# The last feed-forward of a four-layer network as one stage, with its low-rank corrections as products of 32 rows

## The reference

```
even = lt[:, ::2, :]; odd = lt[:, 1::2, :]              # lt: tokens 1 to 16 of each batch
m1 = (even[:, :4, :, None] * odd[:, :4, None, :]).reshape(Bx, Hx, Dx)   # Hx = 1024, Dx = 256
m2 = (even[:, 4:, :, None] * odd[:, 4:, None, :]).reshape(Bx, Dx, Hx)
h = x @ W1.T + scale * einsum('bsd,bhd->bsh', x, m1) + b1
h = gelu(h, approximate=False)
out = h @ W2.T + scale * einsum('bsh,boh->bso', h, m2) + b2
```

## Time and profile before

| | us |
|---|---|
| median of 3 runs | 4879.96 (4879.55 to 4884.21) |
| profiled execution | 4880.05 |
| its span | 4878.3 |
| busy in the span: TensorE / VectorE / ScalarE / GpSimd | 4319.7 / 2473.7 / 1964.9 / 553.3 |

### The profile page before, as it was taken

How to read it: one execution, slowest core, us unless ns; L and a number is a source line. 1 busy time by engine, 2 the same in 40 slices (tenths; PEclk the granted TensorE clock), 3 DMA queues, 4 the chain that set the end, 5 groups by cost and what they waited for, 6 DMA issues and landing times. The chain is left out here.

```text
span 4878.3 us, 144357 instructions
## 1 busy us (share of the span) xinstructions
PE 4319.7 (89%) x65736; PEld 3428.9 (70%) x65736; DVE 2473.7 (51%) x4177; ACT 1964.9 (40%) x3848; POOL 553.3 (11%) x262
## 2 busy tenths in 40 slices
PE   7999996599999979999986789999962789999968
PEld 5877774488888858888853568777741668888844
DVE  4555553566666655545545445555525255555530
ACT  3554442233333334444432335455431244444421
POOL 1111111000000011111112011111102011111100
PEclk9999997599999989999988799999975899999989
DMA  2111100021111121111022011111012611111000
GB/s 69 43 36 43 36 23 16 24 77 49 49 49 49 39 63 37 37 44 37 31 54 53 19 52 43 36 43 36 30 25 84 224 57 38 41 40 38 24 20 19
DMA packets 89472, 223.14 MB, mean 46 GB/s; under 512 B 28736, under 2 KB 52307, under 8 KB 86147
## 3 DMA queue, kind: packets, MB, share of 16 engines
q1 hardware_dynamic: 85360, 209.06, 13.6%
q10 hardware_dynamic: 2736, 2.75, 0.2%
q0 software_dynamic: 768, 2.10, 0.1%
HBM read 196.16 MB, written 9.32 MB: 42 GB/s over the span
## 5 line engine op out<-in xcount | busy, mean ns | idle before, releaser
L690 DVE TENSOR_REDUCE x_pm<-banks 128x4 f32<-128x1536 f32 (+2 forms) x512 | 935.5, 1827 | 687.2 <-PE banks L591 687.2
L792 ACT ACTIVATE x_pl<-banks 128x384 f32<-128x384 f32 x1536 | 628.8, 498 | 710.1 <-PE banks L574 710.1
L516 POOL TENSOR_TENSOR x_cl<-xnT,x_ch 128x1601 fp32r<-128x1601 f32 x116 | 386.4, 3331 | 2171.9 <-ACT x_ch L807 2171.9
L797 ACT ACTIVATE x_kT<-banks,x_bk 128x384 f32<-128x384 f32 (+2 forms) x512 | 305.1, 596 | 530.9 <-PE banks L602 530.9
L614 PE MATMUL banks<-x_wh,x_ch 128*128 128x256 f32 (+1 forms) x1664 | 489.6, 294 | 0.0
L574 PE MATMUL banks<-x_q,x_kT 32*128 32x128 f32 x13312 | 481.8, 276 | 3.1 <-issue 3.0
L591 PE MATMUL banks<-x_kT,x_q 32*128 32x384 f32 (+2 forms) x4096 | 457.8, 512 | 14.0 <-DVE x_v L722 9.0
L614 PE MATMUL banks<-x_wh,x_cl 128*128 128x256 f32 (+1 forms) x1664 | 468.4, 281 | 0.0
L614 PE MATMUL banks<-x_wl,x_ch 128*128 128x256 f32 (+1 forms) x1664 | 467.0, 281 | 0.0
L602 PE MATMUL banks<-x_ch,x_wh 128*128 128x384 f32 (+2 forms) x1024 | 410.3, 401 | 43.7 <-DVE x_cl L773 43.1
L574 PEld LDWEIGHTS banks<-x_q,x_kT 32*128 32x128 f32 x13312 | 435.7, 184 | 6.9 <-issue 4.3
(11 more groups left out here) (339 smaller groups left out, 7010.5 us busy)
## 6 DMA issues: line engine op xcount, KB each, us to landing
xnT<-in_ctxT SPq DMA_DIRECT2D x120, 800.5 KB, 4.3
e_w<-in_L_pack SPq DMA_DIRECT2D x91, 384.0 KB, 3.1
e_w<-in_L_pack SPq DMA_DIRECT2D x21, 1154.0 KB, 7.8
a_swap<-a_raw SPq DMA_DIRECT2D x64, 128.0 KB, 2.3
actT<-in_ctxT SPq DMA_DIRECT2D x8, 800.5 KB, 4.9
e_rw<-routed_rows SPq DMA_DIRECT2D x64, 64.0 KB, 2.8
x_rows<-e_zero SPq DMA_DIRECT2D x1, 2688.0 KB, 9.6
e_xt<-x_rows ACTq DMA_DIRECT2D x3, 896.0 KB, 10.5
```

The lines of the kernel that those rows point to most:

```text
L516: nc.gpsimd.tensor_tensor(cl[:, u, k, 0:CTX], staged(b, k), ch[:, u, k, 0:CTX], ALU.subtract).then_inc(low_done, 1)
L690: nc.vector.tensor_reduce(pm[:, c, :, g], src[:, :, 0:hi - lo], AX.X, ALU.max).then_inc(max_done, 1)
L792: nc.scalar.activation(probabilities(c, j, lo, hi).rearrange("p t q -> p (t q)"), mine[j][:, 0:(hi - lo) * P], ACT.Exp).then_inc(exp_done, 1)
L797: nc.scalar.activation(kT[:, c, lo:hi], mine[1 if g == 0 and inside(b if c else b - 1) else 0][:, 0:hi - lo], ACT.Identity, bias=col[:, c: ...
```

## The change

The two stages and `project` are replaced by one, `lora_ffn`. Instead of 64 rows (all batches) per correction, the 8 batches of a half of the tokens take 32 rows, and four copies of these rows are held side by side in the 128 partitions, one for each of the four products that follow one another: four hidden chunks in the first correction, four token tiles in the second. Each copy meets another 32 rows of TensorE and another bank. The hidden tiles are done in four groups of four (half of the tokens, four chunks). The left side of the second correction is gathered tile by tile, in products that write 32 partitions each; its right side, e2, is made by products with columns of the identity instead of a strided copy. All transfers are issued at the start of the stage, and TensorE waits for the first weights alone before its first plain products. POOL clears two tiles of picks first, since VectorE fills only parts of them.

Left out below: VectorE makes four more picks for c1 after those for e1, and c1 itself as before (128 rows x 512 for each half, after e1); it then fills `pick_e2` and `pick_g` with 16 copies of 32 columns each, the second set behind the e2 drains; for each half it makes `gm` (128x128) and adds the finished tiles. TensorE waits for `g_taken` before the outputs of a half, and issues 4 transposes and 4 products of 512 columns at the start. The stores are as before.

```diff
-def project(net, tag, w, bias, chunks, extra, out):
-def lora_hidden(net, tag, gm, e2):
+def lora_ffn(net, tag, out):
...
+        pick_e1 = net.sb(tag + "_pe1", [P, 2, KC, P], ctx=mem)
+        pick_c = net.sb(tag + "_pc", [P, 2, KC, P], ctx=mem)
+        pick_e2 = net.sb(tag + "_pe2", [P, 2, 4, KC, P], ctx=mem)
+        pick_g = net.sb(tag + "_pg", [P, 2, 4, KC, P], ctx=mem)
...
+        def hidden_bank(h, g, x):
+            return net.bank(4 * (1 - g) + x)
+        def out_bank(t):
+            return net.bank(4 + t if t < 4 else (1, 2, 3, 4)[t - 4])[:, 0:D]
...
+        def _(sp):
+            sp.dma_start(w1[:], d["L3_ffn_W1T"].rearrange("(c p) n -> p c n", p=P)).then_inc(w1_in, 16)
+            sp.dma_start(b1[:], d["L3_ffn_b1"]).then_inc(table_in, 16)
+            sp.dma_start(scale[:], spread(d["L3_ffn_scale"], (P, 1))).then_inc(table_in, 16)
+            sp.dma_start(own[:], d["own_rows"]).then_inc(table_in, 16)
+            sp.dma_start(own8[:], d["own_tile"]).then_inc(table_in, 16)
+            sp.dma_start(m4[:], d["m4"]).then_inc(table_in, 16)
+            sp.dma_start(b2[:], spread(d["L3_ffn_b2"], (P, D))).then_inc(bias_in, 16)
+            sp.dma_start(w2[:], d["L3_ffn_W2T"].rearrange("(c p) n -> p c n", p=P)).then_inc(w2_in, 16)
...
+        def _(pool):
+            nc.gpsimd.memset(pick_e2[:], 0.0).then_inc(cleared, 1)
+            nc.gpsimd.memset(pick_g[:], 0.0).then_inc(cleared, 1)
+            pool.wait_ge(bias_in, 16)
+            for t in range(TILES):
+                nc.gpsimd.tensor_tensor(net.x[:, t, :], net.x[:, t, :], b2[:], ALU.add).then_inc(biased, 1)
...
+        def _(dve):
+            for h in range(2):
+                for c in range(KC):
+                    src = token_rows(c, 1, h).unsqueeze(1)
+                    nc.vector.tensor_copy(pick_e1[:, h, c].rearrange("p (x b i) -> p x b i", x=4, i=4),
+                                          spread(src, (P, 4, 8, 4))).then_inc(ev_picked, 1)
...
+            dve.wait_ge(table_in, 80)
+            dve.wait_ge(ev_made, 1)
+            for h in range(2):
+                for i in range(4):
+                    nc.vector.tensor_scalar(e1[:, h, i], net.bank(0)[:, h * D:(h + 1) * D], m4[:, i:i + 1], None,
+                                            ALU.mult).then_inc(e1_ready, 1)
...
+            for n, (pick, first, picked) in enumerate(((pick_e2, 9, e2_picked), (pick_g, 10, g_picked))):
+                dve.wait_ge(cleared, n + 1)
...
+                if n == 0:
+                    dve.wait_ge(e2_made, 1)
+                    for i in range(4):
+                        nc.vector.tensor_scalar(e2[:, :, i], net.bank(3)[:, 0:2 * S].rearrange("p (h j) -> p h j", h=2),
+                                                m4[:, i:i + 1], None, ALU.mult).then_inc(e2_ready, 1)
...
+        def _(pe):
+            def hidden(h, g):
+                for x in range(4):
...
+                    for k in range(KC):
+                        nc.tensor.matmul(hidden_bank(h, g, x), w1[:, k, c * P:(c + 1) * P],
+                                         net.xnT[:, k, h * HALF:(h + 1) * HALF], start=(k == 0), stop=False)
+                if h == g == 0:
+                    pe.wait_ge(e1_ready, 8)
+                    pe.wait_ge(c_taken, 2)
+                for x in range(4):
+                    c = 4 * g + x
+                    rows = slice(32 * x, 32 * x + 32)
+                    nc.tensor.matmul(hidden_bank(h, g, x), e1[rows, h].rearrange("p i d -> p (i d)")[:, c * P:(c + 1) * P],
+                                     c1[rows, h], start=False, stop=True).then_inc(made, 1)
+            def gates(h):
+                pe.wait_ge(taken, 8 * h + 8)
+                for r in range(4):
+                    for c in range(KC):
+                        for q in range(4):
...
+                            last = nc.tensor.matmul(net.bank(0)[rows, 0:P], pick_g[:, h, r, c, rows],
+                                                    net.actT[:, 2 * r + c, t * P:(t + 1) * P], start=(r == c == 0),
+                                                    stop=(r == 3 and c == KC - 1))
+                last.then_inc(g_made, 1)
+            def outputs(h):
...
+                    nc.tensor.matmul(out_bank(t), gm[rows, h], e2[rows, h].rearrange("p i j -> p (i j)"), start=True, stop=False)
+                for t in range(4 * h, 4 * h + 4):
+                    for c in range(8):
+                        last = nc.tensor.matmul(out_bank(t), net.actT[:, c, t * P:(t + 1) * P], w2[:, c], start=False, stop=(c == 7))
+                    last.then_inc(p_made, 1)
...
+            pe.wait_ge(ev_picked, 4)
...
+            pe.wait_ge(w1_in, 16)
+            hidden(0, 0)
+            pe.wait_ge(e2_picked, 16)
...
+                        last = nc.tensor.matmul(net.bank(3)[:, at:at + 32], pick_e2[:, h, r, c], net.ident[:, r:P:4],
+                                                start=(r == 0), stop=(r == 3))
+            last.then_inc(e2_made, 1)
+            pe.wait_ge(e2_ready, 4)
+            hidden(0, 1)
+            hidden(1, 0)
+            pe.wait_ge(g_picked, 16)
+            gates(0)
+            pe.wait_ge(g_taken, 1)
+            hidden(1, 1)
+            pe.wait_ge(w2_in, 16)
+            outputs(0)
+            gates(1)
+            outputs(1)
```

More of the change, by code:

```diff
@@ L2110, in lora_hidden @@
         b1 = net.sb(tag + "_b1", [P, 8], ctx=mem)
[L2111 to L2118, removed]
+        b2 = net.sb(tag + "_b2", [P, D], ctx=mem)
@@ new lines, in _ @@
+            for t in range(TILES):
+                sp.wait_ge(added, t + 1)
+                sp.dma_start(out[t * P:(t + 1) * P, :], net.x[:, t, :]).then_inc(stored, 16)
+            sp.wait_ge(stored, 16 * TILES)
+        @block.gpsimd
+        def _(pool):
+            nc.gpsimd.memset(pick_e2[:], 0.0).then_inc(cleared, 1)
+            nc.gpsimd.memset(pick_g[:], 0.0).then_inc(cleared, 1)
+            pool.wait_ge(bias_in, 16)
+            for t in range(TILES):
+                nc.gpsimd.tensor_tensor(net.x[:, t, :], net.x[:, t, :], b2[:], ALU.add).then_inc(biased, 1)
@@ new lines, in _ @@
+        @block.vector
+        def _(dve):
[6 more added lines that the diff above has]
+                for c in range(KC):
+                    src = token_rows(c, 2, h).unsqueeze(1)
+                    nc.vector.tensor_copy(pick_c[:, h, c].rearrange("p (x b i) -> p x b i", x=4, i=4),
+                                          spread(src, (P, 4, 8, 4))).then_inc(c_picked, 1)
+            dve.wait_ge(table_in, 80)
+            dve.wait_ge(ev_made, 1)
+            for h in range(2):
+                for i in range(4):
+                    nc.vector.tensor_scalar(e1[:, h, i], net.bank(0)[:, h * D:(h + 1) * D], m4[:, i:i + 1], None,
+                                            ALU.mult).then_inc(e1_ready, 1)
+            for h in range(2):
+                dve.wait_ge(c_made, h + 1)
+                nc.vector.scalar_tensor_tensor(c1[:, h], net.bank(1 + h), scale[:, 0:1], own[:], ALU.mult,
+                                               ALU.mult).then_inc(c_taken, 1)
+            for n, (pick, first, picked) in enumerate(((pick_e2, 9, e2_picked), (pick_g, 10, g_picked))):
+                dve.wait_ge(cleared, n + 1)
+                for h in range(2):
+                    for c in range(KC):
+                        for r in range(4):
+                            dst = pick[:, h, r, c].rearrange("p (q x) -> p q x", x=32)[:, :, 8 * r:8 * r + 8]
+                            src = token_rows(c, first, h).rearrange("p (q b) i -> p q b i", b=2)
+                            nc.vector.tensor_copy(dst.rearrange("p q (b i) -> p q b i", i=4), src).then_inc(picked, 1)
+                if n == 0:
[3 more added lines that the diff above has]
+                                                m4[:, i:i + 1], None, ALU.mult).then_inc(e2_ready, 1)
+            for h in range(2):
+                dve.wait_ge(g_made, h + 1)
+                nc.vector.scalar_tensor_tensor(gm[:, h], net.bank(0)[:, 0:P], scale[:, 0:1], own8[:], ALU.mult,
+                                               ALU.mult).then_inc(g_taken, 1)
+                for t in range(4 * h, 4 * h + 4):
+                    dve.wait_ge(p_made, t + 1)
+                    dve.wait_ge(biased, t + 1)
+                    nc.vector.tensor_tensor(net.x[:, t, :], net.x[:, t, :], out_bank(t), ALU.add).then_inc(added, 1)
@@ new lines, in gates @@
+            def gates(h):
+                pe.wait_ge(taken, 8 * h + 8)
+                for r in range(4):
+                    for c in range(KC):
+                        for q in range(4):
+                            t = 4 * h + q
+                            rows = slice(32 * q, 32 * q + 32)
+                            last = nc.tensor.matmul(net.bank(0)[rows, 0:P], pick_g[:, h, r, c, rows],
+                                                    net.actT[:, 2 * r + c, t * P:(t + 1) * P], start=(r == c == 0),
```

(47 more changed lines are left out.)

39 lines of the change are left out of this document (26 added, 13 removed).

## The result

| | us |
|---|---|
| the changed kernel, median of 4 runs | 4834.35 (4826.34 to 4836.19) |
| the kernel before, 4 runs beside it | 4882.09 (4879.55 to 4889.40) |
| ratio | 0.9901 (95% interval 0.9889 to 0.9913) |
| profiled execution after | 4833.99, span 4832.2 |

A forecast was written before the change was run, and what follows sets the result against it. TensorE's own instructions and holes were taken to bound the stage; 2.9 + 32.1 + 4.7 + 5.1 + 28.8 + 1.7 = 75.3 us against 126.4, so 4880 - 51 = 4829 us, range 4822 to 4840 (own range 4825 to 4834).

The forecast's parts named there:

- Step 1: Start of the stage: POOL's clears hold up VectorE's picks, so TensorE starts 2.9 us later than before.
- Step 2: Ahead of the first layer: TensorE's hole of 4.08 us goes, with the slow first four records (3.51 for 1.71).
- Step 3: Hidden tiles with packed 32-row corrections: 8.03 us a group, 32.1 us for four, where the old took 49.3.
- Step 4: Making e2 by thin products: 3.5 us, then 1.2 us waiting for VectorE's drains, 4.7 us in all.
- Step 5: Gathering the second correction's left side: twice 2.55 us, 5.1 in all, against 13.95 plus a hole of 9.42.
- Step 6: Outputs, second layer with its corrections: 14.4 us for each half, 28.8 in all, against 49.0.
- Step 7: Behind e2's thin products and their hole: one spell at the half clock, +1.7 us, bounds 0 and +5.
- Rival B: Narrow products of corrections and gathering overlap badly: 4851 us with nothing overlapped, 4840 with half; chance 0.17.
- C: TensorE gets the half clock for most of the stage: 4894 us with all work doubled; chance 0.01.
- Rival A: No blocking of picks at the start and no lost clock: 4824 us; chance 0.2.

The follow-up runs named there:

- e1: The changed kernel with POOL's two clears held back until VectorE has made its first eight picks; 4828.20 us, 0.9895 of the kernel before.
- e3: The changed kernel with TensorE's wait for the four e2 drains moved behind the plain products of three hidden tiles; 4830.99 us, ratio 0.9893.
- e2: The changed kernel with the four corrections of a hidden group all read from partitions 0 to 31, one row group; 4845.50 us, ratio 0.9924.
- e5: The changed kernel with each gathering group ordered token tile by token tile instead of the four tiles in turn; 4834.57 us, one run.
- e8: The changed kernel with its bias and second weights asked for only when the last hidden group is made; 4838.19 us, one run.
- e4: The kernel before, with only the second weights and their bias loaded in the first of the two stages; 4872.15 us, ratio 0.9975.

## Why the prediction was right, step by step

- **Step 1, start.** Forecast 2.9 us later than before, by POOL's clears. Measured: TensorE starts 3.86 us after the first pick instead of 1.00, 2.86 later; e1 shows that this was the clears, not the copies. The transposes and small products themselves took 6.11 us instead of 5.74, as the clock rose later (the granted clock was 0.50 for the first 4.1 us of them, before the change for about 3.3): +0.4, not forecast; in e1 they took 5.75.
- **Step 2, first hole.** Gone: plain products follow the small ones without idle time, and the tables (VectorE began at 4752.00) and c1 (done at 4756.5) were there 4.9 us before TensorE asked at 4761.4.
- **Step 3, hidden products.** Forecast 8.03 a group; measured 6.87 + 1.07, then 7.06 or 7.13 + 1.07, 32.4 us for four without the slow spell; forecast 32.1.
- **Step 4, e2.** 3.71 and a hole of 1.2: 4.9 against 4.7.
- **Step 5, gates.** Forecast 2.55 each; 1.93 and 0.42 (0.36 for the drain and the two hand-overs), 2.4.
- **Step 6, outputs.** Forecast 14.4; 14.44 and 14.74. The first half's corrections follow other 32-row products and need no change of width ahead of them.
- **Step 7, clock.** One spell came where it was counted, and its size was off: 2.9 us lost (9.92 for 7.06) against 1.7. The prediction gave thin products and the hole behind them together as the reason; e3 shows that the hole is not needed. I counted a spell like that of the earlier trace rows; its cost varies from execution to execution (1.5 to 2.9 us in the hidden group), and what sets it stays open.

Sum forecast from the first pick: 82.1 us (4741.7 to 4823.8); measured 84.05. Of the missing 1.95, 1.2 are step 7, 0.4 step 6, 0.3 each steps 1 and 3, 0.2 step 4, less 0.4 in step 5. The other 2.85 us between 4829 and the profiled 4833.99 lie ahead of the stage and are no effect of the change that these runs could show. So the whole time is a weaker witness than the stage: the median of 4834.35 is inside the stated range but 0.35 us above the forecast's own range of 4825 to 4834, and the same stage begun at 4737.0 or at 4747.3 us, the first and the last start seen, would have given about 4826 or 4837, an estimate. Rival B is ruled out by the rows of after and by e2 and e5, which show what it would have looked like; C by a granted clock of 1.00 over the last 51 us. Rival A named two things that could be absent; both were present.

By the rule of a semaphore tail (the Trainium skill, TensorE: Matmul & The Clock Gate, "The cost: per-tile semaphore tail") groups with four increments should be 0.08 us longer than with one, an estimate. A hidden group measured 1.07 us against 0.97 for the one-increment form of the earlier trace rows: the size fits, but the products behind differ too, and no run here separates the two. The rule of the shared port (the Trainium skill, SBUF — State Buffer, "Who interferes with whom") held in both halves: the picks waited for POOL, and the eight e1 operations, which read PSUM, took 3.23 us beside POOL's adds (4752.00 and 4752.28 in the rows of after), 0.40 each. In e8, where POOL did nothing at that time, they took the same:

```profile
4746.40 3.23 DVE L2130 TENSOR_SCALAR lf_e<-banks,lf_m 128x256 f32<-128x256 f32 x8 [2.10 <-DMA lf_m<-in_m]
```

## What to carry to other kernels

Low-rank products that leave most rows or columns of TensorE idle are worth copying side by side, but the gain is in the order: neighbours in the instruction stream must lie in different row or column groups, else the same work took three times as long here (3.62 us for 1.07 in e2, 5.90 for 1.93 in e5). Products with few columns are better put between wide ones than in a block: in these kernels that saved the slow spell, 1.5 to 2.9 us. A GpSimd clear that is needed late should not be issued at the moment when VectorE copies between SBUF tiles on the critical path (3.81 us for 0.64).

## What the runs showed of the hardware that I had not expected

- The length of a hole does not tell by itself whether a slow spell follows. In e4 a hole of 1.86 us was followed by one that cost 1.7 us on the first tile, beginning 2 us after TensorE had resumed; a hole of 3.37 us in the same execution and the 0.47-us waits of the changed kernel were followed by none. I had taken holes under 2 us as free.
- The cost of the spell varies, not only its occurrence: 1.5, 2.3, 2.3, 2.8, 2.9 and 2.9 us lost in the same hidden group in six executions with the block and the hole ahead of it (e8, e1, e2, the changed kernel again, the changed kernel, e5). In e1 and e2 the clock fell before the block had ended, which cost 0.5 and 2.1 us more inside it; so the fall needs no idle time at all.
- Sixteen copies of 32 columns take 1.45 us alone (e8, whose bias comes late) and between 2.5 and 3.0 us under POOL's adds (2.54 in e5, 2.99 in the repeated changed kernel): a stall by contention that stayed hidden until the start was made faster.
